# Graph and expert layers on one core: gathers drained at every sixth pair, three PSUM buffers for picked pairs, one bank for turns and logits

## What is computed

```python
def _graph_conv_max(x, src, dst, W_rel, b, W_root):
    agg = jax.ops.segment_max(x[src], dst, num_segments=N)      # N = 1250, 41250 edges, D = 512
    agg = jnp.where(jnp.isfinite(agg), agg, 0.0)
    return agg @ W_rel.T + b + x @ W_root.T
...
h = relu(_graph_conv_max(layernorm(x), ..., W1_rel, b1, W1_root))
h = relu(_graph_conv_max(h, ..., W2_rel, b2, W2_root))
x = x + h
...
probs = softmax(layernorm(x) @ Wr, axis=0)                      # 8 experts, 512 places each
vals, idx = top_k(probs.T, 512)
h = gelu(einsum('ecd,edf->ecf', x_flat[idx], W1) + b1)          # F = 256
out_e = einsum('ecf,efd->ecd', h, W2) + b2
output = zeros.at[idx].add(vals * out_e)
x = x + output
```

## Time and profile before

| | us |
|---|---|
| median of 3 runs | 944.09 |
| lowest, highest | 943.99, 945.03 |
| span of the profiled execution | 1025.1 |
| busy in it: PE, DVE, POOL, ACT | 726.0, 681.6, 546.7, 270.3 |
| gathers in it (372 at L838), busy | 389.5 |
| picked matmuls in it (1200 at L1165), busy | 306.8 |
| granted clock of TensorE, mean | 0.884 |

### The profile page before, as it was taken

How to read it: one execution, slowest core, us unless ns; L and a number is a source line. 1 busy time by engine, 2 the same in 40 slices (tenths; PEclk the granted TensorE clock), 3 DMA queues, 4 the chain that set the end, 5 groups by cost and what they waited for, 6 DMA issues and landing times.

```text
span 1025.1 us, 9702 instructions
## 1 busy us (share of the span) xinstructions
PE 726.0 (71%) x2541; PEld 329.5 (32%) x2541; DVE 681.6 (66%) x1232; ACT 270.3 (26%) x389; POOL 546.7 (53%) x537
## 2 busy tenths in 40 slices
PE   0317555778378778866488657887698678789996
PEld 0214222333133323322133323333243235344442
DVE  3768565588758767873888774898588879733120
ACT  0264250222022202222434030343243122012222
POOL 5652326557746675764556655566447200565644
PEclk9757877899789989987899878998899889899999
DMA  5715336557746675656657756666566400377656
GB/s 136 219 36 183 101 97 184 162 170 214 216 116 194 184 218 144 202 168 184 174 177 214 226 163 180 189 213 193 158 193 187 143 12 1 113 235 142 105 102 82
DMA packets 64770, 162.18 MB, mean 158 GB/s; under 512 B 16383, under 2 KB 20755, under 8 KB 64709
## 3 DMA queue, kind: packets, MB, share of 16 engines
q0 software_dynamic: 40448, 124.74, 44.6%
q1 hardware_dynamic: 17004, 17.16, 6.0%
q10 hardware_dynamic: 7272, 19.74, 5.9%
HBM read 143.37 MB, written 18.11 MB: 158 GB/s over the span
## 4 chain that ended last, share of the span: by engine, by line
PE 33%; DVE 25%; issue 19%; another core or an unknown queue 9%; ACT 5%; POOL 3%; DMA 2%; DVEq 2%; POOLq 0%; ACTq 0%; SPq 0%
PE pp L1165 8%; DVE acc L891 6%; PE prow L1136 5%; PE pp L1563 5%; DVE weights L902 5%; PE pp L1576 4%; PE prow L1103 3%; PE prow L1124 2%; DVE mem L1403 2%; POOL mem L838 1%; DMA mem<-tab,ic 1%; PE pp L1346 1%; PE prow L519 1%; PE pp L501 1%
## 5 line engine op out<-in xcount | busy, mean ns | idle before, releaser
L838 POOL DMA_INDIRECT mem<-tab,ic x372 | 389.5, 1047 | 266.9 <-issue 136.5
L1165 PE MATMUL pp<-weights,slots 128*128 128x512 bf16 x1200 | 306.8, 405 | 114.8 <-DVE acc L891 70.2
L891 DVE TENSOR_TENSOR acc<-acc,pp 128x1024 f32<-128x1024 f32 x180 | 219.1, 1217 | 85.3 <-PE pp L1165 33.5
L1165 PEld LDWEIGHTS pp<-weights,slots 128*128 128x128 bf16 x1200 | 118.0, 103 | 307.5 <-issue 103.8
L902 DVE TENSOR_TENSOR weights<-weights,mem 128x1024 f32<-128x1024 f32 x129 | 158.1, 1226 | 17.9 <-DVE weights L902 11.3
L1136 PE MATMUL prow<-weights,aggT 128*128 128x512 f32 x160 | 92.2, 708 | 37.4 <-ACT aggT L1213 20.5
L1124 PE MATMUL prow<-weights,rootT 128*128 128x512 f32 x160 | 76.0, 619 | 0.0
L1615 POOL DMA_INDIRECT out<-mem,node_of x28 | 44.2, 1577 | 47.3 <-ACT mem L1593 40.9
L1544 DVE COPY weights<-prow 128x512 f32<-128x512 f32 x28 | 18.7, 688 | 72.1 <-PE prow L1103 71.7
L1604 POOL DMA_INDIRECT mem<-xnd,slot_of x20 | 22.0, 1099 | 78.4 <-DVE weight_of L1538 72.6
L1213 ACT ACTIVATE aggT<-prow 128x512 f32<-128x512 f32 x20 | 11.9, 597 | 192.5 <-PE prow L1103 98.7
(11 more groups left out here) (349 smaller groups left out, 828.0 us busy)
## 6 DMA issues: line engine op xcount, KB each, us to landing
slots<-ttd ACTq DMA_DIRECT2D x20, 640.0 KB
mem<-tab,ic POOLq DMA_INDIRECT x372
weights<-in_L_ffn_W SPq DMA_DIRECT2D x9, 512.0 KB, 5.1
weights<-in_L_ffn_W ACTq DMA_DIRECT2D x7, 512.0 KB
xnd<-xin ACTq DMA_DIRECT2D x10, 256.0 KB
mem<-in_x SPq DMA_DIRECT2D x2, 1120.0 KB
tab<-mem SPq DMA_DIRECT2D x1, 2240.0 KB
weights<-in_L_gnn_W_rel SPq DMA_DIRECT2D x2, 1024.0 KB
```

Of the source, the lines that this page charges most:

```text
L838: g.indirect_dma_start(ring[:, h * PAIR + k, :], None, tables[l], bass.IndirectOffsetOnAxis(ic[:, j * PAIR + k:j * PAIR + k + 1], 0))\
L891: v.tensor_tensor(acc[:, :, :], acc[:, :, :], pp[j % 2][:, :, :], ALU.max).then_inc(S["pa"], 1)
L1165: ins = t.matmul(pp[j % 2][:, i, :], sel[u][:, j * KP + i, :], hot[:, j, w, :], start=w == 0, stop=w == 2)
```

## The change

- `gathers`: for each first pair of a half of the loop (`h == 0`, so one pair in six) the value that `ready` has to reach is `j + FLYING` in place of `j + 1`: all pairs before it have landed. The other five of six wait as before.
- A third buffer for picked pairs: the first two banks of `prow`, which were `pt0` and `pt1`. Pair number `k * PAIRS + j` stands in buffer number modulo 3, and its matmuls wait for VectorE's use of the pair three before it.
- In the layers own rows, aggregates, normalized rows and logits are all turned into `pl`. The aggregate of the last tile of layer 0 now waits until ScalarE has copied the turned rows of the next layer's first tile, and those of layer 1 wait until the logits of the tile before have been copied.

No engine gets or loses an instruction that works on data, and their order stays as it was; waits, their values and the banks differ.

```diff
@@ build @@
         ph, po = ([pp[i][:, u, :] for u in range(2)] for i in range(2))
+        buffers = [pp[0][:, :, :], pp[1][:, :, :], prow[:, 0:1024].rearrange("p (u d) -> p u d", u=2)]
@@ gathers @@
-                g.wait_ge(S["ready"], base_g + i * LAP + (j + 1))
+                g.wait_ge(S["ready"], base_g + i * LAP + (j + FLYING if h == 0 else j + 1))
@@ pe_pair @@
-                v.tensor_tensor(acc[:, :, :], acc[:, :, :], pp[j % 2][:, :, :], ALU.max).then_inc(S["pa"], 1)
+                v.tensor_tensor(acc[:, :, :], acc[:, :, :], buffers[(k * PAIRS + j) % 3], ALU.max).then_inc(S["pa"], 1)
@@ first_three @@
-                v.tensor_tensor(acc[:, :, :], in_ring(lo), pp[0][:, :, :], ALU.max).then_inc(S["pa"], 1)
+                v.tensor_tensor(acc[:, :, :], in_ring(lo), buffers[k * PAIRS % 3], ALU.max).then_inc(S["pa"], 1)
@@ root @@
-                four(pt0, own_row[k % NQ], "rT")
+                four(pl[:, :], own_row[k % NQ], "rT")
@@ neighbours @@
                 t.wait_ge(S["fin"], k + 1)
-                four(pt1, agg, "aT")
+                if k == NQ - 1:
+                    t.wait_ge(S["rTe"], NQ + 1)
+                if k > NQ:
+                    t.wait_ge(S["lge"], k - NQ)
+                four(pl[:, :], agg, "aT")
@@ turn_rows @@
-                four(pt0, xin, "nT")
+                four(pl[:, :], xin, "nT")
@@ pairs @@
-                    if j > 1 or k:
-                        t.wait_ge(S["pa"], k * PAIRS + (j - 1))
+                    if j > 2 or k:
+                        t.wait_ge(S["pa"], k * PAIRS + (j - 2))
...
-                            ins = t.matmul(pp[j % 2][:, i, :], sel[u][:, j * KP + i, :], hot[:, j, w, :],
+                            ins = t.matmul(buffers[(k * PAIRS + j) % 3][:, i, :], sel[u][:, j * KP + i, :], hot[:, j, w, :],
                                            start=w == 0, stop=w == 2)
```

More of the change, by code:

```diff
@@ L1003, in vec_tile @@
                     v.wait_ge(S["pairs"], 1)
-                    v.tensor_copy(acc[:, :, :], pp[0][:, :, :]).then_inc(S["pa"], 1)
+                    v.tensor_copy(acc[:, :, :], buffers[0]).then_inc(S["pa"], 1)
                     for j in range(1, PAIRS):
@@ L1207, in own_rows @@
                 a.wait_ge(S["rT"], k + 1)
-                a.activation(rootT[:, :, :].rearrange("p c m -> p (c m)"), pt0, ACT.Copy).then_inc(S["rTe"], 1)
+                a.activation(rootT[:, :, :].rearrange("p c m -> p (c m)"), pl[:, :], ACT.Copy).then_inc(S["rTe"], 1)
             def aggregate(k):
                 a.wait_ge(S["aT"], k + 1)
-                a.activation(aggT[:, :, :].rearrange("p c m -> p (c m)"), pt1, ACT.Copy).then_inc(S["aTe"], 1)
+                a.activation(aggT[:, :, :].rearrange("p c m -> p (c m)"), pl[:, :], ACT.Copy).then_inc(S["aTe"], 1)
             def hidden_rows(q):
@@ L1262, in turned @@
                 a.wait_ge(S["nT"], q + 1)
-                a.activation(own_row[q], pt0, ACT.Copy).then_inc(S["nTe"], 1)
+                a.activation(own_row[q], pl[:, :], ACT.Copy).then_inc(S["nTe"], 1)
                 a.wait_ge(S["lg"], q + 1)
```

## The result

| | us |
|---|---|
| before, median of the timed runs (lowest, highest) | 944.48 (943.99 to 945.03) |
| after, median of 4 runs (lowest, highest) | 999.68 (996.84 to 1004.62) |
| ratio, 95% interval | 1.060, 1.056 to 1.064 |
| forecast | 960, range 943 to 978 |

The sign was forecast and the size was not: the change costs 55 us where 16 were expected.

What follows compares the result with a forecast made beforehand. VectorE was taken to set the pace of quiet tiles, with GpSimd having slack. From 944.1 us, drains added 18.5 (13.5 in layer 0, 5 in layer 1), the third buffer -2, the shared bank 0: 960.6, rounded to 960, range 943 to 978.

Steps and rivals of the forecast that it cites:

- What bounds the kernel before: Quiet tiles: VectorE sets the pace, 26.5 us with 9 pairs plus 1.4 per further pair; GpSimd waits and has slack.
- The price of a drain: GpSimd's gathers: each of 30 full drains delays the next gather by 2.45 us, between zero and 3.4.
- the upper bound I had given: Highest price of one drain at GpSimd's gathers, for a landing behind other traffic: 3.4 us.
- rival 1: Drains absorbed by GpSimd's 108.8 us of waits for ring slots: 942 to 946 us, chance 0.13.
- The lead: GpSimd's usable lead of three ring pairs, 9.3 us, taken off layer 0's 22.8 us shortfall, leaving +13.5 us.
- the hedge: Layer 1's drain cost, taken as 5 us, between 1.8 with the lead taken off and 8.6 in the heavy tile.
- The third buffer: TensorE's picked pairs: waits that go are felt in six tiles of 11 or 14 pairs, credited -2 us.
- Rival 4: One longer TensorE idle time lowers its clock in the chain behind: 4.6 us in up to 18 tiles, 1000 us, chance 0.04.
- The shared bank: Turned rows, aggregates, inputs and logits in one bank: new waits stay covered, 0 us; without cover 3 us.
- The signs that I had named: Changes expected in the trace after: GpSimd's waits, heavy and small tile lengths, TensorE's waits, VectorE's 1.68 us wait.
- Rival 3: Gathers become the outright bound, each drain costing 3.4 us: 985 us, or 973 with half of it, chance 0.14.

Runs made afterwards that it cites:

- before_light: Kernel before with half of VectorE's maximum over gathered ring pairs left out: 906.15 us, ratio 0.959 to the kernel before.
- before_look: Kernel before, unchanged, profiled in a set where it takes 944.63 us, for undisturbed rows: 942.12 us (one run).
- after_b: The changed kernel itself, run again where the kernel before takes 943.8 us: 999.85 us, ratio 1.059.
- drain_only_b: Kernel before with only the drain line added, run where the kernel before takes 943.8 us: 1000.91 us, ratio 1.060.
- third_only_b: Changed kernel without the drain (third buffer and shared bank alone), where the kernel before takes 943.8 us: 963.09 us, ratio 1.020.
- third_fill: Changed kernel without the drain, plus eight unread matmuls ahead of TensorE's wait for the aggregate: 946.81 us, ratio 1.002 to the kernel before.

## Why the prediction was wrong

**What bounds the kernel before: right.** VectorE sets the quiet pace (`before_light`), the quiet tile of 9 pairs takes 26.5 us also in the undisturbed profile, 27.8 in layer 1. The layers' nine tiles are 254.5 and 269.1 us rather than 246.9 and 258.6: the heavy tile is 3 us longer than 1.4 us a pair makes it, and tiles with 7 or 8 pairs are up to 2.5 us longer.

**The price of a drain: the first step that failed.** I took 2.45 us from the earlier trace rows, by letting GpSimd issue at the moment at which VectorE starts on the landed pair. The landing was right (2.75 us after the issue in the earlier trace rows, 2.89 above). What was left out is that GpSimd, once stopped, starts 0.8 to 0.95 us after its release. It does so for either kind of release: in `before_look` VectorE frees a slot at 197.37 and GpSimd starts at 198.25.

```profile
198.25 1.35 POOL L838 DMA_INDIRECT mem<-tab,ic  x1 [2.34 <-DVE weights L902]
...
196.15 1.22 DVE L902 TENSOR_TENSOR weights<-weights,mem 128x1024 f32<-128x1024 f32 x1
```

Over the 30 places of `after_b` the median gap is 3.69 us and the mean 4.00, so the price is 3.4 us at the median and 3.7 on average, against 2.45. The median is at the upper bound I had given (3.4), but I had given it for another reason, landings behind other traffic, and to it a chance of 0.14. The rule of the Trainium skill that spoke for a lower price (DMA: Bandwidth & Descriptors, the anatomy of one GpSimd DMA: 2.0 us and the bytes over 436 GB/s, 2.6 us for 256 KB as an estimate) I had counted from the start of the last issue. The trace gives 3.2 us at the least and 3.7 at the median from there to the landing, over all 372 gathers of after, and 2.7 at the median from the issue's end. The measurement decides: the rule's outcome, rival 1, did not come.

**The lead: the second step that failed.** I took 9.3 us off for the three pairs that GpSimd may be ahead. At the ends of layer 0's tiles it is 2.5 to 5 pairs ahead before and 0.5 to 4 after, but the layer's last pair must be gathered in both kernels before VectorE can finish, and VectorE finishes 10.4 us after the last gather's end before and 7.4 after: 3 us are to be had, not 9.3. The same 3 us in layer 1, where I had taken 5 from between 1.8 and 8.6 us.

The trace's own sum, `after_b` against `before_look`: the 30 places pause for 111 us beyond the usual 0.30 us each. Of these, 48 us take the place of pauses that GpSimd made anyway. The gathers' two stretches are 62 us longer, VectorE finishes 3 us closer behind each, and so the nine tiles grow by 34.0 and 22.6 us, 56.6 in all. My own sum with a price of 3.3 us and no lead comes out near it, at 2.69 + 3.3 / 6 = 3.24 us a pair, 281.9 us for 87 pairs and 35.0 and 23.3 us over VectorE's 246.9 and 258.6. That is in part luck: with the mean price and VectorE's measured tiles it gives 33 and 19 us. By that sum, of the 39.7 us by which the forecast missed, the lead and the hedge make 15.4 (22.8 + 11.1 against 18.5), the price 24.4 (58.3 against 33.9), and the 2 us credited to the third buffer come on top; the three make 41.8, 2 us too many. The idle time that was to absorb the drains was misread as well: GpSimd's 108.8 us of waits for slots (rival 1) are 39 us where no completion is late.

**The third buffer: wrong in sign, by itself.** I credited it with 2 us; alone it costs 19, together with the shared bank. Rival 4 had the mechanism, place and rows (the chain behind the aggregate at the lower clock), and got 0.04, since the quiet tile held 1.00 with waits of 1.28 us. But I had not worked out what the new gap would be: the pairwise waits of before (0.89 + 0.72 + 0.63 = 2.24 us) make up most of the 2.79 us that were measured; the rest isn't accounted for. Its size was too high: 1.7 us in the quiet tile, not 4.6, because the clock is back at 1.00 by 286.50 and the second half product and the fourth pair run at it. In the changed kernel it shows in single tiles. The 9 pairs from 383.3 on take 28.2 us there too (26.5 in `drain_only_b`), and VectorE waits ahead of the third and the fourth pair:

```profile
383.39 0.65 PE L1104 MATMUL pl<-ident,agg 128*128 128x128 f32 x4 [2.80 <-DVE agg L984]
...
389.74 1.22 DVE L892 TENSOR_TENSOR acc<-acc,pp 128x1024 f32<-128x1024 f32 x1 [1.44 <-PE pp L1170]
392.75 1.22 DVE L892 TENSOR_TENSOR acc<-acc,prow 128x1024 f32<-128x1024 f32 x1 [1.79 <-PE prow L1170]
```

Over a layer the gathers set the time, so this isn't added to it: `after_b` and `drain_only_b` differ by 0.1%. The Trainium skill (TensorE: Matmul & The Clock Gate, HAM oscillation) says of a kernel whose TensorE waits for a DMA in every turn of its loop that it falls to the lower clock each time. `third_only_b` agrees, with a wait for VectorE (0.50 behind 2.79 us of idle time), and so does `third_fill`, where a gap of 1.07 us leaves it at 1.00.

**The shared bank: nothing speaks against it.** `third_fill`, which has it, stands at 1.002 (1.000 to 1.004); by itself it wasn't measured.

**The signs that I had named.** Waits for landings should rise to 60 to 75 us; they are 122.9. Waits for slots under 50: 8.7. Heavy tiles 5 to 9 us longer: 15.6 in layer 0, 8.2 in layer 1. Tiles with 7 or 8 pairs should stay: they grew in layer 0, one with 8 pairs from 25.3 to 28.6 us, and hardly in layer 1. TensorE's waits for VectorE's L891 should fall: from 107 to 44. VectorE's 1.68 us ahead of the fourth pair should stay: 1.79, with a new wait ahead of the third. Rival 3, the gathers as the outright bound, was nearest: its price of 3.4 us a drain is the measured median, and its 985 us are too low because it kept the lead.

## What to carry to other kernels

To cost a full drain of a DMA queue, take the last issue's end to the consumer's start on that data, add the restart of the issuing engine as the trace shows it behind any other wait, and spend slack only once per stretch that has to end with its own last transfer. Waiting for all but one pair cost a third of it or less at the median, in sets in which drains hardly showed. If an added buffer lets an engine run ahead, ask where its short waits go: if they merge into one gap ahead of a chain that is waited for, give that gap work (here the third picked pair, 1.5% faster) or keep the waits. And take slack from a profile whose span agrees with the timed runs.

## What the hardware showed that I had not expected

- GpSimd's issue of a gather takes 946 ns unless VectorE is in an operation with two operands in SBUF when it begins; then it mostly ends 0.82 us (median) after that operation (82 of the 99 that began beside L903 in `after_b` took over 1000 ns). Beside maxima that read PSUM it takes 945. Halving those operations made the gathers 21 us shorter in all (396.4 to 375.3). The Trainium skill (SBUF — State Buffer, SBUF: two separate sides) has this stall, as one in which GpSimd waits for VectorE's operation to end; the trace agrees in 104 of the 108 long issues.
- After a wait GpSimd starts 0.87 us (median, for a slot freed by VectorE) or 0.94 us (for a landing) after what released it.
- One idle time of 2.79 us of TensorE is followed by 0.50 of granted clock, and waits of 0.6 to 0.9 us between pairs by 1.00; eight matmuls that nobody needs were worth 17 us.
- The same kernel takes 944 us in some sets and 1032 to 1051 in others, with late completions of TensorE; there the drains, which cost 6% elsewhere, cost 1.4%.
